# Second norm's sums with the y evictions and its squares on ScalarE, lower halves of the routed weights on VectorE, other schedule positions

## The reference, cut to what matters

```python
# 1 tokens
fwd, bwd = ewma(x, 0.1), ewma(x reversed, 0.1) reversed
h = ((fwd + bwd) / 2) @ W.T + b                       # 128 -> 256
# 2 two layers of a selective scan over the 750 steps of each item, 64 states
hidden = layernorm(h)
for l in 0, 1:
    delta = softplus(hidden @ Wd[l] + bd[l])
    u     = hidden @ Wi[l] + bi[l]
    state = scan(state * exp(-delta * softplus(A_log[l])) + delta * u)
    y     = state @ Wo[l] + bo[l]
    hidden = y + (last state @ Ws[l] + bs[l])         # the class row, one per item
h = h + hidden
# 3 feed-forward on z = layernorm(h)
shared = (silu(z @ sg.T) * (z @ su.T)) @ sd.T         # 256 -> 512 -> 256
scores = sigmoid(z @ router.T)                        # 16 experts in 4 groups
best 2 groups by (scores + correction), best 4 experts in them, weights normalised
routed = sum over the 4 experts of weight * (silu(z @ gate_e) * (z @ up_e)) @ down_e   # 256 -> 64 -> 256
out = h + shared + routed
```

## Time and profile before

| | before |
|---|---|
| median of 3 runs | 1284.79 us (1282.39 to 1287.78) |
| profiled execution, its own time | 1284.94 us |
| its span | 1281.3 us |
| mean granted clock of TensorE | 0.968 |
| busy: TensorE / weight loads | 1204.0 (94%) / 1090.0 us (85%) |
| busy: VectorE / ScalarE / GpSimd | 920.8 (72%) / 557.6 (44%) / 403.4 us (31%) |

### The profile page before, as it was taken

How to read it: one execution, slowest core, us unless ns; L and a number is a source line. 1 busy time by engine, 2 the same in 40 slices (tenths; PEclk the granted TensorE clock), 3 DMA queues, 4 the chain that set the end, 5 groups by cost and what they waited for, 6 DMA issues and landing times.

```text
span 1281.3 us, 25554 instructions
## 1 busy us (share of the span) xinstructions
PE 1204.0 (94%) x7874; PEld 1090.0 (85%) x7874; DVE 920.8 (72%) x2361; ACT 557.6 (44%) x913; POOL 403.4 (31%) x282
## 2 busy tenths in 40 slices
PE   6899888988999989998999899998999999999997
PEld 6778777777998889988988799978998899899997
DVE  7775979689668984789678985799578745644453
ACT  2624632552455434563366335553366343223332
POOL 2032172043312623144402423153302431262323
PEclk8978988998999999999999999999999999999999
DMA  4121020122121423231221313231321321243331
GB/s 127 40 68 42 17 78 31 46 78 67 13 54 32 105 51 54 43 83 51 38 67 36 97 33 54 43 98 39 54 48 41 88 35 39 56 108 58 54 53 18
DMA packets 88291, 71.53 MB, mean 56 GB/s; under 512 B 39671, under 2 KB 82848, under 8 KB 88168
## 3 DMA queue, kind: packets, MB, share of 16 engines
q1 hardware_dynamic: 58832, 43.30, 12.4%
q0 software_dynamic: 26832, 26.06, 12.3%
q10 hardware_dynamic: 2504, 0.55, 0.2%
HBM read 31.36 MB, written 39.34 MB: 55 GB/s over the span
## 4 chain that ended last, share of the span: by engine, by line
PE 67%; DVE 21%; issue 6%; ACT 3%; POOL 2%; DMA 0%; DVEq 0%; POOLq 0%; ACTq 0%
PE gu_ps L1798 18%; PE gu_ps L1767 14%; PE d_ps L1874 10%; PE d_ps L1855 8%; PE ch_ps L1744 3%; PE ch_ps L1842 3%; PE ch_ps L1834 1%; DVE h L1532 1%; DVE h L1264 1%; PE ch_ps L1670 1%; PE ch_ps L1730 1%; PE ch_ps L1688 1%; DVE stats L1270 1%; PE ch_ps L1700 1%; DVE gu_ps L1521 1%
## 5 line engine op out<-in xcount | busy, mean ns | idle before, releaser
L853 POOL DMA_INDIRECT out_dram<-block_rows,entry x99 | 158.1, 1597 | 323.6 <-ACT block_rows L1013 303.2
L1798 PE MATMUL gu_ps<-gu_hi,bx_hi 128*128 x792 | 234.9, 297 | 3.6 <-issue 3.6
L1001 ACT ACTIVATE hid<-gu_ps 128x512 f32<-128x512 f32 (+1 forms) x195 | 115.2, 593 | 270.7 <-PE gu_ps L1798 172.7
L1798 PE MATMUL gu_ps<-gu_lo,bx_hi 128*128 x792 | 225.5, 285 | 0.0
L1798 PE MATMUL gu_ps<-gu_hi,bx_lo 128*128 x792 | 225.1, 284 | 0.0
L834 POOL DMA_INDIRECT lists<-records,pos x96 | 126.4, 1317 | 191.3 <-DVE pos L1429 165.8
L1855 PE MATMUL d_ps<-down,hid 128*125 128x256 f32 x768 | 182.6, 381 | 0.0
L1798 PEld LDWEIGHTS gu_ps<-gu_hi,bx_hi 128*128 128x128 f32 x792 | 151.6, 191 | 9.4 <-issue 8.6
L1855 PEld LDWEIGHTS d_ps<-down,hid 128*125 128x125 f32 x768 | 139.1, 188 | 18.5 <-issue 0.3
L1798 PEld LDWEIGHTS gu_ps<-gu_hi,bx_lo 128*128 128x128 f32 x792 | 151.7, 192 | 0.8
L1798 PEld LDWEIGHTS gu_ps<-gu_lo,bx_hi 128*128 128x128 f32 x792 | 151.2, 191 | 0.0
(11 more groups left out here) (290 smaller groups left out, 2928.0 us busy)
## 6 DMA issues: line engine op xcount, KB each, us to landing
block_rows<-lists SPq DMA_DIRECT2D x99, 128.0 KB, 2.9
out_dram<-h SPq DMA_DIRECT2D x24, 500.0 KB
t<-rstd_scratch SPq DMA_DIRECT2D x21, 250.0 KB, 5.0
x_in<-in_x_dram SPq DMA_DIRECT2D x8, 375.0 KB, 7.6
zt<-in_x_dram SPq DMA_DIRECT2D x7, 375.0 KB, 3.8
entry<-lists SPq DMA_DIRECT2D x99, 8.0 KB, 2.6
out_dram<-block_rows,entry POOLq DMA_INDIRECT x99, 3.9
lists<-records,pos POOLq DMA_INDIRECT x96, 4.2
```

What stands on the lines that cost most here:

```text
L853: pool.indirect_dma_start(out=out_rows[0:there, :], out_offset=bass.IndirectOffsetOnAxis(entry[n % UE][:, ID:ID + 1].bitcast(U32), 0), in_ ...
L1001: inc(act.activation(hid[g % 4][:, 0:n], gu_ps[:, 2 * (g % 2), 0:n], ACT.Silu), "silu_done")
L1798: last = pe.matmul(gu_ps[:, 2 * (g % 2) + half, q * GH:(q + 1) * GH], a[n % 2][:, k, :], w[:, k, bass.ds(of, 1), half * GH:(half + 1) * GH ...
```

## The change

Four things are changed.

1. A y step evicts its two token tiles one by one with an operation that also writes out the sum of each token's 256 values (`hsum`). The two bn_stats are gone.
2. A new step `ln2_sq` on ScalarE squares (hsum - 256 h) of each of four token tiles and writes out the sum (`hsq`), behind the third's second y step. `ln2_stats` on VectorE waits for it and is one operation of 125 x 4 in place of seven. The squares themselves go into `records`, which is overwritten by the norm afterwards.
3. The lower halves of the six parts of the routed weights go from GpSimd to VectorE, and the upper halves stand at other ticks.
4. Many positions in CHAIN, EARLY and PREPARE are others, so the order of instructions on each engine changes.

```diff
 CHAIN = (
-    ("ewma", 1, dict(SP=-27.0, DVE=-28.0, POOL=-27.0, ACT=-27.0)),
+    ("ewma", 1, dict(SP=-28.5, DVE=-31.0, POOL=-27.0, ACT=-27.0)),
-    ("ewma_back", 1, dict(DVE=-27.5)),
+    ("ewma_back", 1, dict(DVE=-29.5)),
...
+    ("ssm_decay", 1, dict(DVE=-9.5, ACT=-8.5)),
     ("pre", (1, 1), dict(PE=-12.0, DVE=-12.0, ACT=-11.5)),
-    ("ssm_decay", 1, dict(DVE=-9.5, ACT=-9.0)),
...
-    ("split", (1, 0), dict(ACT=-7.5, DVE=-7.0)),
+    ("split", (1, 0), dict(ACT=-7.0, DVE=-7.0)),
-    ("residual", 1, dict(DVE=-4.5)),
+    ("residual", 1, dict(DVE=-5.0)),
...
     ("y", (0, 1), dict(PE=-5.0, DVE=-4.5)),
-    ("split", (1, 1), dict(ACT=-6.5, DVE=-7.0)),
+    ("ln2_sq", 0, dict(ACT=-4.5)),
+    ("split", (1, 1), dict(ACT=-6.5, DVE=-6.5)),
     ("residual", 2, dict(DVE=-4.5)),
     ("ln2_stats", 0, dict(DVE=-4.5, POOL=-4.0)),
     ("y", (1, 0), dict(PE=-4.5, DVE=-4.5)),
     ("ln2_norm", 0, dict(DVE=-4.0, ACT=-4.0)),
     ("residual", 3, dict(DVE=-4.0)),
     ("y", (1, 1), dict(PE=-4.0, DVE=-4.0)),
-    ("ln2_norm", 1, dict(DVE=-2.0, ACT=-1.5)),
+    ("ln2_sq", 1, dict(ACT=-4.0)),
+    ("ln2_norm", 1, dict(DVE=-1.5, ACT=-1.5)),
...
-    ("x2t", (1, 0), dict(PE=0.0, ACT=0.0, DVE=0.0)),
+    ("x2t", (1, 0), dict(PE=-0.5, ACT=-0.5, DVE=-0.5)),
...
     ("y", (2, 1), dict(PE=-0.5, DVE=-0.5)),
+    ("ln2_sq", 2, dict(ACT=-0.5)),
...
-    ("route_pick", 0, dict(DVE=7.5)),
+    ("route_pick", 0, dict(DVE=8.5)),
...
-    ("table", 3, dict(DVE=17.0)),
+    ("table", 3, dict(DVE=16.5)),
...
 EARLY = {
...
-    (1, "ln1_part", 1): dict(DVE=-24.0),
+    (1, "ln1_part", 1): dict(DVE=-25.0, POOL=-24.0),
...
+    (0, "ewma", 0): dict(SP=-30.5),
+    (1, "ln2_norm", 0): dict(ACT=-4.5),
+    (1, "rstd_row", 1): dict(PE=-23.4, ACT=-23.8),
+    (1, "ln1_stats", 0): dict(DVE=-24.0, POOL=-25.5),
 }
...
 PREPARE = (
-    (2.4, "routed", 0), (4.9, "routed", 1), (7.4, "routed", 2),
-    (10.9, "routed", 3), (11.4, "routed", 4), (11.4, "routed", 5),
+    (0.4, "routed", 0), (1.4, "routed", 1), (2.4, "routed", 2),
+    (9.9, "routed", 3), (11.4, "routed", 4), (11.4, "routed", 5),
+    (1.6, "routed_low", 0), (2.6, "routed_low", 1), (3.1, "routed_low", 2),
+    (22.4, "routed_low", 3), (26.4, "routed_low", 4), (27.4, "routed_low", 5),
 )
...
 # GpSimd
             def prepare(what, n):
-                if what == "routed":
-                    hi_p, lo_p = routed_parts[n]
-                    pool.wait_ge(S["routed_hi"], n + 1)
-                    inc(pool.tensor_tensor(lo_p, lo_p.bitcast(F32), hi_p.bitcast(F32), ALU.subtract), "routed_lo")
+                pass
...
 # ScalarE
+                elif step == "ln2_sq":
+                    wait(act, "y_ev", 6 * pair + 2 * arg + 2)
+                    wait(act, "aggr2", NT * (pair - 1) + arg + 1)
+                    wait(act, f"list_st{arg}", 16 * SUB * pair)
+                    wait(act, "x2t_mm", 6 * (pair - 1) + 2 * arg + 2)
+                    for j in range(arg * SUB, (arg + 1) * SUB):
+                        last = act.activation(records[:, j, 0:D], h_of[pair % 2][:, j, :], ACT.Square,
+                                              bias=hsum[:, j:j + 1], scale=-float(D), accum_out=hsq[:, j:j + 1])
+                    inc(last, "sq2")
...
 # VectorE
+                elif what == "routed_low":
+                    hi_p, lo_p = routed_parts[n]
+                    dve.wait_ge(S["routed_hi"], n + 1)
+                    inc(dve.tensor_tensor(lo_p, lo_p.bitcast(F32), hi_p.bitcast(F32), ALU.subtract), "routed_lo")
...
 # ln2_stats
-                        wait(dve, "st2", SUB * (done + 1))
-                        wait(dve, "xn2", done)
-                    variances(stats[n], halves[n], mv[n], f"aggr{n + 1}", NAGGR * done)
+                        wait(dve, "sq2", NT * pair + arg + 1)
+                        wait(dve, "rstd2", NT * pair + arg)
+                        inc(dve.tensor_scalar(var[:], hsq[:, arg * SUB:(arg + 1) * SUB], 1.0 / (D * D * D), EPS,
+                                              ALU.mult, ALU.add), "aggr2")
...
 # ln2_norm
-                    inc(dve.scalar_tensor_tensor(nmr[:], mv[1][:, :, 0], -1.0, rstd[1][:], ALU.mult, ALU.mult), "nmr")
+                    inc(dve.scalar_tensor_tensor(nmr[:], hsum[:, arg * SUB:(arg + 1) * SUB], -1.0 / D, rstd[1][:],
+                                                 ALU.mult, ALU.mult), "nmr")
...
 # y
-                    inc(dve.tensor_tensor(hv, ch(step, arg, pair)[0:TP, :].rearrange("p (j d) -> p j d", d=D), hv,
-                                          ALU.add), "y_ev")
-                    wait(dve, "y_ev", 6 * pair + 2 * t + q + 1)
-                    if q == 0:
-                        wait(dve, "aggr2", NAGGR * (NT * pair + t))
+                    wait(dve, "sq2", NT * (pair - 1) + t + 1)
                     for n in range(2):
-                        inc(dve.bn_stats(stats[1][:, 2 * q + n, :], hv[:, n, :]), "st2")
+                        last = dve.scalar_tensor_tensor(hv[:, n, :], ch(step, arg, pair)[0:TP, n * D:(n + 1) * D], 1.0,
+                                                        hv[:, n, :], ALU.mult, ALU.add,
+                                                        accum_out=hsum[:, j + n:j + n + 1])
+                    inc(last, "y_ev")
```

More of the change, by code:

```diff
@@ L230 @@
     (-14.4, "fold", 4),
-    (2.4, "routed", 0),
-    (4.9, "routed", 1),
     (-12.4, "shared", 1),
-    (7.4, "routed", 2),
     (-12.4, "shared", 2),
-    (-11.4, "shared", 3),
-    (10.9, "routed", 3),
-    (-11.2, "shared", 4),
-    (11.4, "routed", 4),
-    (11.4, "routed", 5),
+    (-10.4, "shared", 3),
+    (-10.2, "shared", 4),
     (-3.7, "shared", 5),
@@ L243 @@
     (-12.5, "routed_loads", 1),
-    (-3.5, "routed_loads", 2),
+    (-2.5, "routed_loads", 2),
     (-6.0, "routed_loads", 3),
-    (-8.0, "routed_loads", 4),
+    (-11.0, "routed_loads", 4),
     (-1.5, "routed_loads", 5),
+    (0.4, "routed", 0),
+    (1.4, "routed", 1),
+    (2.4, "routed", 2),
+    (9.9, "routed", 3),
+    (11.4, "routed", 4),
+    (11.4, "routed", 5),
+    (1.6, "routed_low", 0),
+    (2.6, "routed_low", 1),
+    (3.1, "routed_low", 2),
+    (22.4, "routed_low", 3),
+    (26.4, "routed_low", 4),
+    (27.4, "routed_low", 5),
 )
@@ L454, in audio_tower_kernel @@
         WIDE = (NJ, SUB)
[L455 to L457 removed]
+        stats = sb("stats1", [TP, NJ, 6])
+        halves = sb("halves1", [TP, NJ, 2])
+        mv = sb("mv1", [TP, NJ, 2])
+        hsum, hsq = (sb(name, [TP, NJ]) for name in ("hsum", "hsq"))
+        var = sb("var2", [TP, SUB])
         rstd = [sb(f"rstd{n + 1}", [TP, w]) for n, w in enumerate(WIDE)]
```

82 lines of the change are left out of this document (41 added, 41 removed).

## The result

The changed kernel takes 1276.25 us (median of nine, 1272.01 to 1281.18) against 1285.13 (median of nine, 1281.97 to 1287.78): ratio 0.9932, 95% interval 0.9911 to 0.9953. That is 8.9 us faster; 21.8 were forecast.

A forecast was written before the change was run, and what follows sets the result against it. TensorE, busy 94% of the span, was taken as the bound, leaving its idle time and slow clock. Savings 10.5 + 3 + 0.8 + 7.5 = 21.8 us from 1284.9 gave 1263 us, range 1248 to 1284.

The forecast's parts named there:

- Second norm: ScalarE: Four squares per third, 2.4 us; VectorE waits 1.7 us once a pair; the other two thirds cost nothing.
- a sum of 0.7: Full pairs: token eviction end 0.7 us earlier after cheaper steps and moved scans, against the 1.7 us wait.
- The five waits: TensorE's token-eviction stalls: 0.7 plus half of 1.7 for slow clock, 1.5 a pair, 7.5 us saved.
- my own first part: What bounds the kernel: in pair 0 VectorE is held while GpSimd makes the routed weights' lower halves.
- Second norm: VectorE: y step 1.0 us, 0.4 saved six times a pair; one variance operation of 0.17, 0.6 saved three times.
- Lower halves: Moved to VectorE: 8.3 us freed in pair 0's chain, of which TensorE can use 3.3.
- The decay behind silu: Layer 1's ssm_decay behind silu: pair 0's 5.9 us wait goes, 2.4 from faster warm-ups; pair 1 gives 3.
- given back: Rival: pair 1's chain has another last link, only 5.9 goes, full pairs lose 0.3 each; 1280 us, chance 0.12.
- The squares' tables: If each group of squares changed tables and back, VectorE's wait would be 4.3 instead of 1.7 us.
- 1303: Time in us of the rival where squares hold VectorE, if they needed table loads; chance 0.11.
- the slower one: Rival: squares hold VectorE, ln2_stats 0 waiting in order; with table changes 1303 us, chance 0.11.
- Early gain only: Rival: pairs 0 and 1 give 13.5, full pairs' squares wait eats the rest, clock falls; 1271 us, within 0.77 forecast chance.

The follow-up runs named there:

- the one run without it: Changed kernel with y (1, 0) ahead of ln2_stats 0 on VectorE; 1274.0 us (one run).
- two places: Changed kernel with last third's squares at tick 0.0, x2t (1, 0) back at 0.0, and y (1, 0) ahead of ln2_stats 0; 1265.9 us, ratio 0.9844.
- second trace: The changed kernel run again, unaltered, for its own spread; 1277.4 us, ratio 0.9919 to the kernel before.
- scan earlier: Changed kernel with the second item's backward scan half a tick earlier, ahead of y (0, 0); 1279.6 us (one run).
- scan later: Changed kernel with both squares and y (1, 0) edits, plus the second item's backward scan at -28.5, behind y (1, 0); 1268.3 us, ratio 0.9846.
- GpSimd earlier: Changed kernel with both squares and y (1, 0) edits, plus GpSimd's part of the first item's average two ticks earlier; 1269.5 us, ratio 0.9855.
- the norm alone: Kernel before with only the second norm's change, all old positions; 1296.6 us, ratio 1.0064.

## Why the prediction was wrong, by its own steps

**Second norm: ScalarE, the step that failed.** It priced the squares (forecast 2.4 us, measured 2.0) only by VectorE's wait (forecast 1.7, measured 1.55), and said that the other two thirds "cost nothing". It listed what stands behind the waiting instruction on VectorE, but not what stands behind the four squares on ScalarE, except a silu. In the same queue stands hid_hi, whose lower half frees a PSUM bank. For the last third that is 1.3 us a pair. For the first third the step named the right victim, y (1, 0)'s bank, and put it inside a sum of 0.7; by the one run without it, it costs 0.9 to 2.1 us a pair by itself. The two together are 12.4 us in the full pairs (changed 706.6, two places 694.2), where the forecast missed 11.6 us (-6.0 against +5.6). By the changed kernel's second trace they are 8.7, where it missed 7.9 (-6.0 against +1.9). By the ratios of all runs they are 9.6 to 11.3 of the 12.9 missed in the whole. The rest is not taken apart; part of it lies in "1 to 2", 4.3 us short, of which the two places give 2.0. In "6 to 7", which had no stall to lose, the price stands bare: 4.5 us, of which the two places take back 3.0, and a wait of 2.2 us for hid_lo stays.

**The five waits.** Stall and slow stretch did go, in all five stretches, which is more than the half I took. Their 4.1 us, seen at the slots right behind the eviction (-3.9 in "1 to 2", -4.1 in each of the four others), went into other waits. I followed one chain to its end and stopped. The banks are two and used in turn, so any late eviction on VectorE can become a wait of TensorE, whatever it is for. The scan's collision with GpSimd was in my own first part as a mechanism for pair 0, and I did not ask it again for the scan that the change moves beside GpSimd's addition. What that collision costs is not shown: none of the three positions tried against it (scan earlier, scan later, GpSimd earlier) gained anything.

**Second norm: VectorE.** Mis-sized to the safe side: a y step takes 0.68 us, not 1.0 (before 1.39), and the variance 0.16 in the median, as forecast (0.17). The Trainium skill, VectorE: DVE Perf Modes, section Two Vector instructions with no wait between them, says an accumulator output makes two instructions; the trace agrees on the two, and the second takes 0.08 us, so my step from it to "nearer 1.4" was wrong.

**Lower halves.** The 8.3 us of VectorE were freed, though the two splits above give 3.4 of them back in the changed kernel, and from slot 3 to slot 11 they gave 4.2 us against 3.3 forecast. Slots 0 to 3 were priced at 0.5 and lost 2.3. In thirteen of the fifteen traces with the upper halves at ticks 0.4 to 2.4 on ScalarE slots 0 to 3 take 15.0 us or more, in two 12.6 and 12.7; without them 12.4 to 12.9. A wait of 1.1 us for x_lo is in the short ones too, but the clock is lower in the long ones, as these two windows from slot 0 to slot 3 show, first of the changed kernel, then of the kernel with lower halves only (PE, PEld, DVE, ACT, POOL busy, granted clock):

```profile
104.50:119.60 15.10, 13.99 (x63) 11.56 (x62) 7.12 (x19) 9.98 (x20) 3.26 (x2) 0.78 0.00 0
```

```profile
106.50:119.10 12.60, 11.50 (x63) 9.53 (x62) 8.28 (x26) 7.90 (x13) 3.29 (x2) 0.96 0.00 0
```

Idle time is equal (1.11 and 1.10), busy time is 2.5 more. Why the clock is lower there stays open.

**The decay behind silu.** Added up with the halves as if separate, 5.9 + 2.4 and 3.3. They share a cause: without GpSimd beside the sum the wait is 2.50 in the old order. In the stretch to 1,0 the single parts give -2.4 (decay) and -3.4 (halves), both -4.9, and the whole change -8.4. Of the 3.5 left the norm alone has 1.0; the other 2.5 come with the other positions, which I had put at nothing, and were not taken apart. So that pair 0 gives 10.3 where 10.5 were forecast is luck in part: the two parts that I priced give 6.4 by themselves, from the start of slot 0 on. For pair 1 the mechanism of the rival "given back", another last link, was right: the wait of 2.10 us went, the class row's product comes after 2.27 idle ones, and from slot 11 to the first block it is 16.4 us in both kernels.

**The squares' tables.** Both traces have 92 table loads, and none stands ahead of a square, so 1303, which rested on them, fell. The Trainium skill, ScalarE: Activation LUTs, section Table sets: the hidden batching unit, leaves square out of its examples of functions in every set; in this trace square behaved like them.

Of the rivals the slower one was right in its place: the norm alone is slower (1.0064). Its mechanism, ln2_stats 0 waiting in order, is one half of it; the other half, the order on ScalarE, no rival had. "Early gain only" was right that the full pairs eat what the cheaper steps give, but the clock did not fall behind the token evictions as before.

## What to carry to other kernels

When work moves to an engine with room, list everything behind it in that engine's queue and ask of each which buffer it gives back: 2 us of squares ahead of a 0.6 us copy cost 1.3 us a pair, and behind it they left no wait. When a stall on one of two alternating banks is removed, follow the next uses of both; most of its 4.1 us came back as waits of 0.8 to 1.8. Two gains that rest on one cause are not added: price each with the other already made.
